# Per-tile waits between indirect row transfers, and a different split of early expert weights over two DMA queues, in a fused MoE–SSM–MoE kernel

## The reference

```
x = x + 0.5 * moe(layernorm(x))
x = x + ssm(layernorm(x))
x = x + 0.5 * moe(layernorm(x))       # the same weights as the first
```

## Time and profile before

| what | value |
|---|---|
| median of 3 runs | 561.29 us (558.7 to 562.9) |
| the profiled execution's own time | 560.26 us |
| its span, first to last instruction | 558.3 us |
| mean granted TensorE clock | 0.984 |
| PE busy (matmul) | 522.4 us, 94% |
| DVE, ACT, POOL busy | 327.4, 157.6, 231.5 us |
| DMA | 67.70 MB, mean 121 GB/s |

### The profile page before, as it was taken

How to read it: one execution, slowest core, us unless ns; L and a number is a source line. 1 busy time by engine, 2 the same in 40 slices (tenths; PEclk the granted TensorE clock), 3 DMA queues, 4 the chain that set the end, 5 groups by cost and what they waited for, 6 DMA issues and landing times. The chain is left out here.

```text
span 558.3 us, 11040 instructions
## 1 busy us (share of the span) xinstructions
PE 522.4 (94%) x4356; PEld 423.1 (76%) x4357; DVE 327.4 (59%) x654; ACT 157.6 (28%) x336; POOL 231.5 (41%) x208
## 2 busy tenths in 40 slices
PE   2999999999978999999998899999999989999995
PEld 2998998448937999546896799884478989954695
DVE  3553335512546999995596699999656522222224
ACT  1111122222117444451311844444221111222210
POOL 1022000220415999992354499999302520000041
PEclk9999999999978999999999999999989999999999
DMA  7999788210305456531221456454101320110021
GB/s 230 398 407 353 275 305 290 69 67 22 95 14 136 119 124 150 148 91 31 93 86 50 126 125 120 134 148 111 30 11 51 105 75 29 39 39 12 19 60 65
DMA packets 41988, 67.70 MB, mean 121 GB/s; under 512 B 5040, under 2 KB 24752, under 8 KB 41936
## 3 DMA queue, kind: packets, MB, share of 16 engines
q1 hardware_dynamic: 31344, 44.69, 27.6%
q10 hardware_dynamic: 7024, 12.19, 6.0%
q0 software_dynamic: 3568, 10.10, 5.4%
HBM read 48.74 MB, written 18.22 MB: 120 GB/s over the span
## 5 line engine op out<-in xcount | busy, mean ns | idle before, releaser
L492 PEld LDWEIGHTS ps<-xt,w_gu 128*128 128x128 f32 x1360 | 161.1, 197 | 11.7 <-ACT xt L746 8.2
L492 PE MATMUL ps<-xt,w_gu 128*128 128x128 f32 x1360 | 165.1, 282 | 4.7 <-ACT xt L746 4.2
L965 DVE SCALAR_TENSOR_TENSOR hb<-hb,ps 128x640 f32<-128x640 f32 x68 | 55.5, 817 | 152.2 <-ACT hb L728 152.0
L517 PE MATMUL ps<-w_dn,hb 128*128 128x256 f32 x520 | 120.7, 379 | 0.0
L517 PEld LDWEIGHTS ps<-w_dn,hb 128*128 128x128 f32 x520 | 94.9, 190 | 10.8
L728 ACT ACTIVATE hb<-ps 128x640 f32<-128x640 f32 x68 | 47.4, 697 | 160.9 <-PE ps L492 148.2
L911 POOL DMA_INDIRECT region<-yg_rows,ypos x32 | 31.0, 968 | 146.0 <-DMA yg_rows<-ob 128.7
L492 PEld LDWEIGHTS ps<-xnt,w_gu 128*128 128x128 f32 x720 | 85.9, 197 | 1.6 <-issue 0.8
L492 PE MATMUL ps<-xnt,w_gu 128*128 128x128 f32 x720 | 86.7, 281 | 0.0
L943 POOL TENSOR_TENSOR xnt<-xnt,hh 128x512 f32<-128x512 f32 x64 | 81.5, 1277 | 0.0
L1010 DVE TENSOR_TENSOR_SCAN ps<-ps,region 128x512 f32<-128x512 f32 x64 | 78.2, 1222 | 0.3 <-POOL region L930 0.2
(11 more groups left out here) (102 smaller groups left out, 321.8 us busy)
## 6 DMA issues: line engine op xcount, KB each, us to landing
bcb<-bc_rows SPq DMA_DIRECT2D x22, 512.0 KB, 5.1
region<-bc_rows SPq DMA_DIRECT2D x10, 512.0 KB, 4.8
xg<-xg_rows SPq DMA_DIRECT2D x34, 128.0 KB
w_gu<-in_wg SPq DMA_DIRECT2D x4, 640.0 KB, 13.2
w_gu<-in_wu SPq DMA_DIRECT2D x4, 640.0 KB, 14.4
w_dn<-in_wd SPq DMA_DIRECT2D x4, 640.0 KB, 16.8
w_gu<-in_wg ACTq DMA_DIRECT2D x4, 640.0 KB, 4.7
w_gu<-in_wu ACTq DMA_DIRECT2D x4, 640.0 KB, 5.7
```

The source lines that it names most:

```text
L492: last = nc.tensor.matmul(gup(p)[:, c * P:(c + 1) * P], w_gu4[:, e, k, c * P:(c + 1) * P], x, start=(k == 0), stop=(k == KC - 1))
L517: ins = nc.tensor.matmul(outp(p), hb[:, p, c * P:(c + 1) * P], w_dn4[:, e, c, :], start=(c == 0), stop=(c == IC - 1))
L965: nc.vector.scalar_tensor_tensor(out=h, in0=h, scalar=1.0, in1=gup(p)[:, 0:I], op0=ALU.add, op1=ALU.mult).then_inc(s_a, 1)
```

## The change

Two independent edits, in `before` and `after`:

1. Each token tile t gets a scatter semaphore of its own (`s_sc[t]`, counted up over the segments), in place of one for each segment. POOL no longer waits once for the first four DMAs of a scatter or gather: ahead of token tile t = 2 it waits for the two DMAs of tile 0, ahead of t = 3 for those of tile 1. Where SP and DVE waited on a segment's one semaphore for all 8 scatters, they now wait on four semaphores (`scattered`).
2. Experts 2 and 3 leave SP's stream. ACT's stream sends expert 2 at the end of its tile 0 and expert 3 at the end of its tile 2; experts 4 to 7 stay at tiles 3 to 6.

```diff
-        s_sc = [sem(f"s_sc{s}") for s in range(SEGS)]
+        s_sc = [sem(f"s_sc{t}") for t in range(TT)]
...
-        N_SC = 2 * TT * 16
-        EARLY = (E + 1, 0, 1, 2, 3)
-        LATE = {3: 4, 4: 5, 5: 6, 6: 7}
+        def scattered(engine, s):
+            for t in range(TT):
+                engine.wait_ge(s_sc[t], 2 * 16 * (s + 1))
+        EARLY = (E + 1, 0, 1)
+        LATE = {0: 2, 2: 3, 3: 4, 4: 5, 5: 6, 6: 7}
...
-                    sp.wait_ge(s_sc[s], N_SC)
+                    scattered(sp, s)
...
                     for t in range(TT):
+                        if t >= 2:
+                            pool.wait_ge(s_sc[t - 2], 2 * 16 * (s + 1))
                         for j in range(2):
                             nc.gpsimd.indirect_dma_start(
                                 out=xg_dram[s % 2],
                                 out_offset=bass.IndirectOffsetOnAxis(ap=pos[:, s, j, t:t + 1], axis=0),
-                                in_=xn["P"][:, t, :], in_offset=None).then_inc(s_sc[s], 16)
-                        if t == TT // 2 - 1:
-                            pool.wait_ge(s_sc[s], N_SC // 2)
+                                in_=xn["P"][:, t, :], in_offset=None).then_inc(s_sc[t], 16)
...
                     for t in range(TT):
+                        if t >= 2:
+                            pool.wait_ge(s_gat[t - 2], 2 * 16 * (s + 1))
                         for j in range(2):
                             nc.gpsimd.indirect_dma_start(
                                 out=gat[:, t, j, :], out_offset=None, in_=yg_dram[s % 2],
                                 in_offset=bass.IndirectOffsetOnAxis(ap=ypos[:, s, j, t:t + 1], axis=0)
                                 ).then_inc(s_gat[t], 16)
-                        if t == TT // 2 - 1:
-                            for u in range(TT // 2):
-                                pool.wait_ge(s_gat[u], 2 * 16 * (s + 1))
...
-                    dve.wait_ge(s_sc[0], N_SC)
+                    scattered(dve, 0)
```

More of the change, by code:

```diff
@@ L433, in _ @@
                     sp.wait_ge(s_rows[1 + h], 16)
-                    sp.wait_ge(s_sc[1 + h], N_SC)
+                    scattered(sp, 1 + h)
                     for m in range(SLOTS):
```

## The result

| | median (us) | lowest to highest | runs |
|---|---|---|---|
| before, same chip | 560.56 | 558.7 to 562.9 | 4 |
| after | 572.76 | 571.26 to 575.77 | 4 |

A forecast was written before the change was run, and what follows sets the result against it. TensorE (PE), busy in nearly every slice, was taken to bound the kernel. Gains of 0.94, 1.25 and 2.06 us made 4.25, so 557.0 against the 561.29 median; 0.5 for clock gave 556.5 us, range 553.8 to 559.6.

The forecast's parts named there:

- Does a pause go away?: POOL's scatters and gathers: in quiet stretches a scatter's pause shrinks from 1.68 to 0.30 us, a gather's from 2.5 to 0.30.
- small terms: Extra SP and DVE waits at `scattered` cost 0 to 0.9 us before a load; other gathers' 2.2 us win nothing.
- rival 4: ACT's weight issues are held, its tanh comes late and PE stands: slower, up to 574.3 us; chance 0.03.
- Segment 3, 2.06 us: PE's wait for loaded routed rows near 454 us goes whole, as gathers and scatter end earlier: gain 2.06 us.
- Segment 2, 1.25 us: POOL leaves the scatter earlier, so the norm's power starts 1.25 us earlier and PE's wait nearly goes: gain 1.25 us.
- Segment 0, 0.94 us: Scatter under full DMA engines: last issue ends 0.94 us earlier, PE still waits 1.10 us; ends -0.67 and 2.04.
- the bad end: Segment 0's scatter: the second weight queue adds 3.22 us to a transfer's delay, last issue 0.67 us later than before.
- The sum: Gains in segments 0, 2 and 3: 0.94 + 1.25 + 2.06 = 4.25 us, so 557.0 against the median of 561.29.
- The clock term: Some removed PE waits are followed by a fall in PE's granted clock; 0.5 us allowed, taking the forecast to 556.5.
- Contention unfelt: Segment 0's wait for routed rows goes whole despite full DMA engines: 1.1 us more gain, 555.4 us; chance 0.24.
- Second queue eats the gain: The second weight queue, on ACT, takes segment 0's gain, the end at -0.67: 558.1 us; chance 0.16.
- Pauses stay: Something other than the four-transfer wait holds POOL, so only scraps are won: 560.5 us; chance 0.07.

The follow-up runs named there:

- chip 12: Round 1's chip: weights edit alone 1.0007, waits edit alone 0.992, new waits in scatters only 0.994, in gathers only 1.001, all against before.
- the waits alone: Edit 1 on before, with the old weights: 554.53 us, ratio 0.992 in round 1; 574.72 us, ratio 1.017 in round 2.
- chip 6: Round 2's chip: after itself 1.022, edit 1 alone 1.017; with new weights, new waits in scatters only 1.002, in gathers only 1.013, against before.
- chip 0: Round 4's chip, against before: new waits in scatters of segments 0, 2, 3 0.996 with either weights, weights edit alone 1.001, waits one tile back 1.042.
- chips 6 and 2: Chips of rounds 2 and 3: after itself 1.022 in round 2; after without any waits between transfers 1.017 in round 3, against before.
- pairs: After with scatters and gathers waiting for the tile one back instead of two back: 584.10 us, ratio 1.042 against before.

## Why the prediction was wrong

**The step that failed** is "Does a pause go away?", in its last sentence: "Behind POOL's new waits stand only its own next issues." As a statement on semaphores that is true, and POOL's pauses shrank: the gathers' to 0.30 us as worked out, the quiet scatters' to 0.61 to 0.88. But I took a pause as time in which nothing useful happens to anyone. It had a second effect that no row of before shows by itself: it let the other engines' streams run. The same omission stands under small terms, where the gathers' 2.2 us "win nothing"; they were put at zero, and they cost 5.4 us of holds in segments 0 to 2 (2.26 + 2.41 + 0.7) and clock besides. Segment 1's scatter, which the sum doesn't name because no PE wait hung on it, cost another 5.4. None of the rivals held this case, so the range was too narrow on the slow side; that rival 4's 574.3 us lies near the measured 572.76 is chance, as its cause (held issues of ACT) didn't occur.

A trace of before did carry a hint: PE has two small "issue" gaps in front of down products in segment 1, 0.48 and 0.39 us, each 5.2 us behind the start of a series of four. They aren't in the traces of chip 12. I read past them because they are under 1 us.

**Segment 3, 2.06 us:** right. The wait is gone, and PE's matmuls stand 2.23 us better at that place. **Segment 2, 1.25 us:** right; 1.47.

**Segment 0, 0.94 us:** right in sign, too high in after: 0.32 us (56.57 to 56.25). With the waits alone, on chip 12, PE's wait is 1.15 us, 0.89 less than before. POOL's last issue came 1.86 us earlier, more than the 0.94 worked out, but the rows were issued 4.99 us behind its end, where before it was 3.59: the delay moved from POOL's pause to the landing of the last transfers. The Trainium skill ("DMA: Bandwidth & Descriptors", "Queues, rings and completion order") has each DMA engine go round its loaded queues; by that I had the last issue 0.67 us later as the bad end. The issue didn't come later. The longer landing can't be put down to the rule either: with the weights in SP's queue alone it is as long (5.28 us with the waits alone on chip 12, 5.05 on chip 6), so a share of one in three wasn't seen here.

**The sum** of 4.25 us is what the waits alone gave on the chip without holds: 558.66 - 554.53 = 4.1 (that kernel lacks the weights' edit, and after itself wasn't run there). The mechanisms that I named were sized well; what I didn't name was worth about 16 us (572.76 less 556.5), of which the ledger of the profiled runs finds 11.6 in holds and some 3.3 in clock.

**The clock term** (0.5 us) was too small: two new stretches at 1.2 GHz cost 1.7 us each, one behind a new wait of PE, the other without one.

**Rivals.** Contention unfelt: no, PE's wait on loaded rows is still 1.77 us. ACT's issues held: no, 0.68 us (27.13). Second queue eats the gain: perhaps in part. On chip 0 PE's first wait for rows is 1.77 us with the new weights and 1.20 with the old, one trace each; on chip 6 it is the other way round (1.59 and 1.99). It is not what made the loss. Pauses stay: no.

**What stays open.** Shown is that the large holds need a series of more than four indirect transfers, come with scatters and gathers, with and without waits on POOL, with either split of weights, and go with a break of 2.45 us. A shorter one may do: in segment 2's scatter of after POOL paused 0.88 us behind four, and nothing was held. Which resource the series takes from the others, nothing here shows. The amount of data isn't it. The DMA view from 100 to 120 us, in after:

```profile
DMA packets 994, 1.60 MB, mean 80 GB/s; under 512 B 224, under 2 KB 736, under 8 KB 992
```

and with the waits alone on chip 12, without holds:

```profile
DMA packets 1184, 1.78 MB, mean 89 GB/s; under 512 B 255, under 2 KB 925, under 8 KB 1181
```

The held one moves less. The loading of instructions doesn't differ either: from 105 to 115 us the queues of kind "instruction" move one packet in each of the two traces. Why chip 12 doesn't hold, with identical code, is open too, and so is whether it would on another day; chips 6 and 2 do, chip 0 does at least mildly, though after itself wasn't run on it.

## What to carry to other kernels

A pause on one engine isn't idle time for the chip: before removing one, look at what the other engines do during it and in the stretch where it won't be any more, and remove it only where an engine on the critical path waits for its end. In this kernel series of about four indirect transfers, with a break of some 2.5 us between them, cost least, and a longer one paid only where an engine on the critical path waited for its end (the scatters of segments 0, 2 and 3, of which only segment 2's then ran as eight in a row); that turned 1.022 into 0.992 to 0.996. When parts taken alone seem harmless and the whole isn't, run the same part again on another chip, and the whole on the first one, before believing in an interaction.

## What the runs showed of the hardware that was not expected

- From some 6 us after the start of a series of six to eight indirect transfers (issued every 1.25 to 1.28 us) until 0.3 to 2 us after its last, PE issues matmuls 0.7 us apart that need no semaphore, and ACT and DVE pass waits that are already met up to 5 us late. "Trainium Architecture — The Big Picture" of the Trainium skill, section "What this means for kernel authors", says that engines are independent processors and that one doesn't block another without a semaphore between them. The traces of chips 6 and 2 and of the first timing disagree (in the last, 9.08 us in place of 5.92 for a tanh, 5.06 for a product), and so does chip 0's for one tanh (7.95). The traces of chip 12 agree.
- Identical code gave a ratio of 0.992 on one chip and 1.017 on another, each outside the other's interval. Each was timed there in one session.
- Three pauses behind pairs cost more (1.042) than no pause at all (1.017), each against before on its own chip.
